# Attention's output projection with fp32 operands instead of split fp16 halves, and the value bias added where the values are spread

## The chip, the cores and the metric

The kernel runs on one core of one Trainium2 chip. The metric is the device time of one launch in microseconds (us), the median of several runs. The engines are named as in the profile: PE (TensorE, its weight loads apart as PEld), DVE (VectorE), ACT (ScalarE), POOL (GpSimd) and SP (SyncE, which here issues all DMAs).

## The reference, cut to what matters

One transformer layer for 32 batch entries of 512 tokens and 256 channels: adaptive layer norm, causal attention with 16 heads of 16 channels and a linear position bias, a gated residual, a second adaptive layer norm, and a gated feed-forward part. The change touches these lines only:

```python
qkv = x @ w_qkv.T + b_qkv
q, k, v = jnp.split(qkv, 3, axis=-1)
...
probs = jax.nn.softmax(scores, axis=-1)
out = jnp.einsum('bhqk,bhkd->bhqd', probs, v)
out = out.transpose(0, 2, 1, 3).reshape(B, S, D)
return out @ w_out.T + b_out
```

The rows of `probs` sum to one, so the value part of `b_qkv` may be added to `v`, or after the division by the softmax sum to the attention's output. The bias is not zero here.

## The kernel before, in words

All 32 batch entries go through one software pipeline written by hand. A batch is called b. One iteration i has 16 slots, one for each head h of batch i, and every engine walks through the same slots in its own instruction stream; semaphores tie the streams together. In iteration i the scores and the exponentials of batch i are made, the row maxima of batch i (heads 8 to 15, slots 0 to 7) and of batch i+1 (heads 0 to 7, slots 8 to 15), the layer norm and QKV product of batch i+1, the output projection of batch i-1 and the feed-forward part of batch i-2. The tables SIDE, SP_AT, DVE_AT, POOL_AT and ACT_AT (L29 to L87) say in which slot each of these side steps stands.

A slot looks like this on the three busiest engines:

- PE (order "01asub2wc", L25): scores in three chunks 0, 1 and 2 (L575, a head's transposed scores for the exponential), row scores in three parts a, b, c (L589, 512, 384+128 and 256 columns, for the row maxima), the side steps s and u, and w, the product of exponentials and values for one key tile of the group of four heads before (L603, L609, fp32).
- DVE (order "SUaboc", L27): the side steps S and U of the slot before, the maxima a and b (L853), the steps o of DVE_AT, then the maxima c.
- ACT: the exponentials (L647) and the evictions of the side products.

The row scores alternate between two PSUM banks (L585), so PE's row scores b of slot t+1 wait until DVE has read the maxima c of slot t (L584), and the row scores c of a slot wait for its maxima a. The side products alternate between two other banks; each waits until the product before it in its bank has been read (L505).

The output projection of batch i-1 is made so. The unnormalised attention output goes through DRAM and comes back as `oc`, the reciprocal sums as `rz`. POOL multiplies them to `om` in slot 9 (`normalise`, L986). In slot 11 ACT writes `oh`, the fp16 rounding of om plus the value bias `bv` (`o_hi`, L714), and DVE writes `ol`, the rest in fp16 (`o_lo`, L868), in its place o, between the maxima b and c. PE makes the product "out" in slots 14 (n = 0) and 15 (n = 1), each with two times six matmuls of 128x128 weights by 256 columns: oh by wo_hi, oh by wo_lo, ol by wo_hi, for two channel halves (L497, called from L548). DVE multiplies it with the gate to `ot` (L799), POOL adds the residual (L1000).

The values: ACT evicts them to `vst` (L684) and POOL spreads them to `va` (`spread`, L976), four heads at a time, into groups of 32 columns of which 16 hold the values and the others the ones for the softmax sum. POOL's order in the slots is: mask of head t (L1018, which zeroes the exponentials above the diagonal), then the steps of POOL_AT: spread of group 2 in slot 1, of group 0 in slot 2, of groups 1 and 3 in slot 3. Ahead of the mask of slot 0 stands norm_c of slot 15 (L965, L969). The step w of slot 4 is the first on head group 0 and waits for the masks of heads 0 to 3 and for a spread (L597 to L599).

Of the kernel before, what the change touches and what calls it, by code (L numbers as in the profile page):

```python
# [7 lines left out]
F32 = mybir.dt.float32  # L8
F16 = mybir.dt.float16
# [5 lines left out]
P = 128  # L15
WS = 16.0
# [48 lines left out]
    11: [("o_lo", None, -1)],  # L65
# [19 lines left out]
    11: [("o_hi", None, -1)],  # L85
# [4 lines left out]
SILU, SILU_T, MOD, ROWS, OW_T, WEIGHTS, MOE = 3, 5, 9, 17, 18, 28, 32  # L90
# [8 lines left out]
def build(nc, x, w_qkv, b_qkv, w_out, b_out, gate_w, expert_w, out_w, cond, wmod,  # L99
# [10 lines left out]
    with ctx:  # L110
# [19 lines left out]
        wo_hi = sb("wo_hi", [P, DC, D], F16)  # L130
        wo_lo = sb("wo_lo", [P, DC, D], F16)
# [5 lines left out]
        bv = sb("bv", [P, DC], F32)  # L137
# [29 lines left out]
        oh = sb("oh", [P, DC, S], F16)  # L167
        ol = sb("ol", [P, DC, S], F16)
# [68 lines left out]
        for name in ("ld_c", "ld_m", "ld_w", "set_dve", "set_pe", "set_act", "set_ready", "rows_stored", "kaug_loaded",  # L237
                     "xa_loaded", "moda_loaded", "lna_stats", "lna_aggr", "lna_ready", "rsa_ready", "xna_ready",
                     "ta_ready", "hfa_ready", "hha_ready", "hla_ready", "qk_ready", "qk_hi", "qk_lo",
                     "qk_stored0", "qk_stored1", "qk_stored2", "qk_stored3", "stack_loaded0", "stack_loaded1",  # L240
                     "stack_loaded2", "stack_loaded3", "masked",
                     "v_ready", "v_evicted", "va_ready", "mx_ready", "mx_read", "mt_ready", "nm_ready",
                     "aug_loaded", "st_ready", "exp_done", "pv_done", "ou_ready", "ou_stored",
                     "zc_loaded", "oc_loaded", "zr_ready", "rz_stored", "rz_loaded", "om_ready", "oh_ready",
                     "ol_ready", "out_ready", "ot_ready", "x1_ready", "xc_loaded", "ga_loaded", "xg_ready",
                     "lnc_stats", "lnc_aggr", "lnc_ready", "rsc_ready", "xnc_ready", "modc_loaded", "gb_loaded",
                     "t2_ready", "hfc_ready", "hhc_ready", "hlc_ready", "gate_ready", "gate_step", "gate_exp",
                     "scl_ready", "moe_ready", "z0_ready", "zs_ready", "zg_ready", "res_ready", "res_stored",
                     "passed_sp", "passed_dve", "passed_pool"):
            sm(name)  # L250
# [63 lines left out]
        def _(sp):  # L314
# [16 lines left out]
            ld("ld_w", bv[:], b_qkv[2 * D:3 * D].rearrange("(c p) -> p c", p=P), allow_slow_non_contiguous=True)  # L331
# [111 lines left out]
        def _(pe):  # L443
# [56 lines left out]
            def side_step(name, n, b, bank, prev):  # L500
# [39 lines left out]
                elif name == "out":  # L540
                    wait(pe, "ol_ready", (b + 1) * 2)
                    for u in range(2):
                        t = slice((2 * n + u) * P, (2 * n + u + 1) * P)
                        pairs = []
                        for c in range(DC):
                            pairs += [(oh[:, c, t], wo_hi[:, c, :]), (oh[:, c, t], wo_lo[:, c, :]),
                                      (ol[:, c, t], wo_hi[:, c, :])]
                        x_ = products(dst[:, u * D:(u + 1) * D], pairs)  # L548
# [88 lines left out]
        def _(act):  # L637
# [71 lines left out]
            def o_hi(b):  # L709
                wait(act, "om_ready", b + 1)  # L710
                wait(act, "out_ready", b * 2)
                wait(act, "ol_ready", b * 2)
                for c in range(DC):
                    nc.scalar.activation(oh[:, c, :], om[:, c, :], ACT.Identity,  # L714
                                         bias=bv[:, c:c + 1]).then_inc(s["oh_ready"], 1)

# [21 lines left out]
            steps = dict(sums_out=sums_out, gate_exp=gate_exp, o_hi=o_hi)  # L738
# [4 lines left out]
        def _(dve):  # L743
# [119 lines left out]
            def o_lo(b):  # L863
                wait(dve, "om_ready", b + 1)
                wait(dve, "oh_ready", b * 2 + 2)
                wait(dve, "out_ready", b * 2)
                for c in range(DC):
                    v.scalar_tensor_tensor(ol[:, c, :], om[:, c, :], bv[:, c:c + 1], oh[:, c, :], ALU.add,  # L868
                                           ALU.subtract).then_inc(s["ol_ready"], 1)

# [5 lines left out]
                invert=invert, o_lo=o_lo)  # L876
# [32 lines left out]
            step(v.tensor_scalar(mrow[:, 0:D], g_abs[:, 0:D], 1.0 / WS, None, ALU.mult))  # L909
# [4 lines left out]
            def split(hi, lo, src):  # L914
# [9 lines left out]
            split(wo_hi[:].rearrange("p c n -> p (c n)"), wo_lo[:].rearrange("p c n -> p (c n)"),  # L924
                  flat[:, 12 * P:16 * P])
# [34 lines left out]
        def _(pool):  # L960
# [11 lines left out]
            def spread(b, g):  # L972

                wait(pool, "v_evicted", (b + 1) * 2, "passed_pool")
                wait(pool, "pv_done", b * 16 - 4 * (3 - g), "passed_pool")
                q.tensor_scalar(va[:, :, 4 * g:4 * g + 4, 0:HD],  # L976
                                vst[:, :, 64 * g:64 * g + 64].rearrange("p t (h d) -> p t h d", h=4),
                                1.0, 0.0, ALU.mult, ALU.add).then_inc(s["va_ready"], 1)

            def normalise(b):  # L980
# [3 lines left out]
                wait(pool, "oh_ready", b * 2, "passed_pool")  # L984
                wait(pool, "ol_ready", b * 2, "passed_pool")
# [90 lines left out]
```

## Time and profile before

| | us |
|---|---|
| median of 3 runs | 1957.38 |
| runs | 1954.21, 1957.84, 1957.38 |
| span of the profiled execution, first to last instruction | 1953.2 |
| granted TensorE clock, mean of the span | 0.977 |
| busy PE / PEld | 1724.6 / 995.6 |
| busy DVE | 1552.6 |
| busy ACT | 1214.8 |
| busy POOL | 998.9 |

The profile shows one execution. Its time with what lies around the span is not listed by itself; the three timed runs lie 1.0 to 4.6 us above its span. A busy PE is not PE at its peak, since a matmul's shown duration contains its way through the array; the distance from one start to the next is what a matmul costs in a dense row. "Idle before" is the time in which an engine did nothing ahead of an instruction, with the instruction that released it.

### The profile page before, as it was taken

The numbers are of one execution on the slowest core, as the hardware profiler recorded it, in microseconds if no ns is written. First come the engines' busy times: TensorE is split into PE (matmuls) and PEld (weight loads), VectorE is DVE, ScalarE is ACT, GpSimd is POOL, SyncE is SP. The second block draws the span as 40 slices with busy tenths as digits, with TensorE's granted clock in tenths as the row PEclk, the third lists the DMA queues.
The fourth block names the chain that finished last, engine by engine and source line by source line (L and its number), as shares of the span: only waits on it lengthen the run. The fifth ranks groups of instructions, "written<-read, shape, count | busy, mean of one in ns | idle before, by whom it ended". The sixth has DMA issues, their size and how long they took to land.

```text
span 1953.2 us, 62334 instructions
## 1 busy us (share of the span) xinstructions
PE 1724.6 (88%) x17744; PEld 995.6 (51%) x17744; DVE 1552.6 (79%) x5632; ACT 1214.8 (62%) x2466; POOL 998.9 (51%) x1225
## 2 busy tenths in 40 slices
PE   5799999998989998999999898999899999999974
PEld 3455555555555455555555555545555555555542
DVE  5778888888888878888888888887888888888843
ACT  1366666666666666666666666666666666666651
POOL 3234555545545455555554554545555545455454
PEclk8799999999999999999999999999999999999986
DMA  4243333433333443333344333344333334433321
GB/s 131 77 133 116 125 119 128 141 128 124 125 104 125 140 136 126 120 125 120 128 141 128 123 125 104 126 141 136 125 120 125 121 129 139 131 123 115 120 88 45
DMA packets 206753, 238.21 MB, mean 122 GB/s; under 512 B 27626, under 2 KB 153138, under 8 KB 206674
## 3 DMA queue, kind: packets, MB, share of 16 engines
q1 hardware_dynamic: 206710, 237.67, 37.3%
q8 instruction: 23, 0.38, 0.1%
q14 instruction: 20, 0.16, 0.0%
HBM read 135.13 MB, written 101.81 MB: 121 GB/s over the span
## 4 chain that ended last, share of the span: by engine, by line
PE 49%; DVE 24%; issue 18%; ACT 4%; DMA 2%; DVEq 2%; POOL 1%; SPq 1%; ACTq 0%; POOLq 0%
PE ps L497 18%; PE ps L589 12%; DVE ps L853 9%; PE ps L575 8%; PE ps L609 4%; PE ps L603 4%; DVE mxt L853 4%; DVE ol L868 2%; DVEq L257 1%; ACT hf_a L658 1%; ACT hh_a L660 1%; DVE qk_st L793 1%; DVE st_c L759 1%; ACT prob L647 1%; PE ps L515 1%
## 5 line engine op out<-in xcount | busy, mean ns | idle before, releaser
L853 DVE CUSTOM_DVE_ANT_0 ps<-ps,mask_qk 128x512 f32<-128x512 f32 (+3 forms) x2048 | 971.1, 510 | 296.3 <-PE ps L589 285.3
L647 ACT ACTIVATE prob<-ps 128x512 f32<-128x512 f32 (+1 forms) x1536 | 743.5, 530 | 363.2 <-PE ps L575 362.3
L589 PE MATMUL ps<-kz,qs 112*128 112x512 f16 (+3 forms) x2048 | 542.4, 307 | 138.2 <-DVE mxt L853 129.5
L1018 POOL TENSOR_SCALAR_AFFINE_SELECT prob<-prob 128x512 f32<-128x512 f32 x512 | 353.4, 696 | 364.2 <-ACT prob L647 364.2
L575 PE MATMUL ps<-qs,kz 114*128 114x128 f16 (+2 forms) x3584 | 453.3, 243 | 3.7 <-DMA qs<-negm 3.1
L589 PEld LDWEIGHTS ps<-kz,qs 112*128 112x128 f16 x2048 | 187.1, 97 | 492.8 <-DVE mxt L853 308.6
L853 DVE DVE_READ_ACCUMULATOR2_ANT mxt<- 128x1 f32 x2048 | 288.6, 141 | 0.0
L575 PEld LDWEIGHTS ps<-qs,kz 114*128 114x128 f16 x3584 | 259.7, 98 | 50.5 <-ACT prob L647 3.8
L609 PE MATMUL ps<-prob,va 128*32 128x384 f32 (+2 forms) x3072 | 237.0, 380 | 0.0
L603 PE MATMUL ps<-prob,va 128*32 128x128 f32 x4096 | 218.3, 285 | 2.0 <-issue 0.9
L679 ACT ACTIVATE qk_st<-ps,bqk 128x512 f16<-128x512 f32 x128 | 88.0, 688 | 97.7 <-PE ps L497 95.7
L992 POOL TENSOR_TENSOR xg<-xc,ga_bc 128x1024 f32<-128x1024 f32 x32 | 75.6, 2361 | 101.6 <-DMA ga_bc<-rows_d 90.5
L986 POOL TENSOR_TENSOR om<-oc,rz 128x1024 f32<-128x1024 f32 x32 | 75.5, 2359 | 95.3 <-DMA rz<-rz_d 95.3
L603 PEld LDWEIGHTS ps<-prob,va 128*32 128x32 f32 x4096 | 81.1, 108 | 84.6 <-issue 81.7
L965 POOL TENSOR_TENSOR rs_c<-ve_c,neg_half 128x4 f32<-128x4 f32 x32 | 32.7, 1022 | 166.4 <-DVE nm_c L774 166.4
L793 DVE SCALAR_TENSOR_TENSOR qk_st<-ps,bqk,qk_st 128x512 f16<-128x512 f32 x128 | 95.6, 747 | 7.1 <-ACT qk_st L679 7.1
L497 PE MATMUL ps<-moe_hi,hh_c 128*128 128x512 f16 x256 | 99.5, 389 | 1.0 <-DVE gsub L826 1.0
L1008 POOL TENSOR_TENSOR zg<-zs,gb_bc 128x512 f32<-128x512 f32 x64 | 81.4, 1271 | 36.1 <-DVE zs L806 35.1
L695 ACT ACTIVATE z<-ps,scl 128x256 f32<-128x256 f32 x128 | 60.5, 473 | 62.9 <-PE ps L497 58.8
L497 PE MATMUL ps<-moe_lo,hh_c 128*128 128x512 f16 x256 | 99.2, 387 | 0.0
L497 PE MATMUL ps<-moe_hi,hl_c 128*128 128x512 f16 x256 | 99.1, 387 | 0.0
L497 PE MATMUL ps<-hh_a,wqkv_hi 128*128 128x512 f16 x256 | 97.9, 382 | 0.4 <-DVE qk_st L793 0.4
(115 smaller groups left out, 2818.7 us busy)
## 6 DMA issues: line engine op xcount, KB each, us to landing
qk_d<-qk_st SPq DMA_DIRECT2D x128, 256.0 KB, 2.0
ou_d<-ou SPq DMA_DIRECT2D x128, 256.0 KB, 2.0
qs<-qk_d SPq DMA_DIRECT2D x128, 192.0 KB, 2.6
kz<-qk_d SPq DMA_DIRECT2D x256, 96.0 KB, 2.6
xa<-in_L_attn_x SPq DMA_DIRECT2D x32, 512.0 KB, 4.3
qk_d<-qk_st SPq DMA_DIRECT2D x128, 128.0 KB, 1.9
xc<-in_L_attn_x SPq DMA_DIRECT2D x32, 512.0 KB, 3.5
oc<-ou_d SPq DMA_DIRECT2D x64, 256.0 KB
```

What stands on the lines that cost most here:

```text
L497: x_ = mm(dst, a, b, start=(n == 0), stop=(n == len(pairs) - 1))
L575: x_ = mm(ps[:, ST + n, col:col + w * P], kz[0:STACK, h, kt * P:(kt + 1) * P], qs[0:STACK, h // 2, qt * P:(qt + w) * P], start=True, stop= ...
L589: x_ = mm(ps[:, bank, col:col + w], qs[0:CONST, h // 2, qt * P:(qt + 1) * P], kz[0:CONST, h, 0:w], start=True, stop=True)
L603: x_ = mm(ps[32 * j:32 * j + 32, PVB, kt * P:(kt + 1) * P], va[:, kt, h, :], prob[:, h % 8, kt * P:(kt + 1) * P], start=(kt == 0), stop=(k ...
L609: x_ = mm(ps[32 * j:32 * j + 32, PVB, (kt + 1) * P:S], va[:, kt, h, :], prob[:, h % 8, PCOL[kt]:PCOL[kt] + w], start=False, stop=False)
L647: nc.scalar.activation(prob[:, h % 8, at:at + w], ps[:, ST + n, 0:w], ACT.Exp, scale=1.0 / FS).then_inc(s["exp_done"], 1)
L679: nc.scalar.activation(qk_st[:, k, 0, :], src, ACT.Identity, bias=bqk[:, 2 * k + n // 2:2 * k + n // 2 + 1]).then_inc(s["qk_hi"], 1)
L793: v.scalar_tensor_tensor(qk_st[:, kk, 1, :], src, bqk[:, 2 * kk + n // 2:2 * kk + n // 2 + 1], qk_st[:, kk, 0, :], ALU.add, ALU.subtract). ...
L853: x_ = v.tensor_tensor_reduce(ps[:, bank, col:col + w], ps[:, bank, col:col + w], mask_qk[:, S - w:S], 1.0, -3e38, ALU.add, ALU.max, mxt[: ...
L992: q.tensor_tensor(xg[:], xc[:], ga_bc[:, 1:2, :].broadcast_to([P, QT, D]), ALU.add).then_inc(s["xg_ready"], 1)
L1008: q.tensor_tensor(zg[:, t, :], zs[:, t, :], gb_bc[:].rearrange("p (o d) -> p o d", o=1).broadcast_to([P, 2, D]), ALU.mult).then_inc(s["zg_ ...
L1018: q.affine_select(out=d, in_=d, compare_op=ALU.is_ge, fill=0.0, base=0, pattern=[[0, 4], [1, P]], channel_multiplier=-1).then_inc(s["maske ...
```

## The change

The output projection takes `om` and a fp32 copy of the weights `wo_f` directly; a product then has two matmuls of fp32 operands in place of six of fp16. The steps o_hi on ACT and o_lo on DVE go, with their tiles and semaphores. PE waits for `om_ready` instead of `ol_ready`; POOL's normalise waits for the product of the batch before (`out_ready`) instead of oh and ol. The value bias is loaded as a row broadcast to all partitions, and spread, a tensor_scalar with one tensor input before, becomes a tensor_tensor that adds this row. At the start, one copy stands for the two steps that split the output weights, and the first gate row is no longer divided by the weight scale.

```diff
-    11: [("o_lo", None, -1)],
...
-    11: [("o_hi", None, -1)],
...
-            ld("ld_w", bv[:], b_qkv[2 * D:3 * D].rearrange("(c p) -> p c", p=P), allow_slow_non_contiguous=True)
+            ld("ld_w", bv_bc[:], b_qkv[2 * D:3 * D].rearrange("(o d) -> o d", o=1).broadcast_to([P, D]))
...
-                    wait(pe, "ol_ready", (b + 1) * 2)
+                    wait(pe, "om_ready", b + 1)
                     for u in range(2):
                         t = slice((2 * n + u) * P, (2 * n + u + 1) * P)
-                        pairs = []
-                        for c in range(DC):
-                            pairs += [(oh[:, c, t], wo_hi[:, c, :]), (oh[:, c, t], wo_lo[:, c, :]),
-                                      (ol[:, c, t], wo_hi[:, c, :])]
+                        pairs = [(om[:, c, t], wo_f[:, c, :]) for c in range(DC)]
                         x_ = products(dst[:, u * D:(u + 1) * D], pairs)
...
-            def o_hi(b):
-                wait(act, "om_ready", b + 1)
-                wait(act, "out_ready", b * 2)
-                wait(act, "ol_ready", b * 2)
-                for c in range(DC):
-                    nc.scalar.activation(oh[:, c, :], om[:, c, :], ACT.Identity,
-                                         bias=bv[:, c:c + 1]).then_inc(s["oh_ready"], 1)
...
-            def o_lo(b):
-                wait(dve, "om_ready", b + 1)
-                wait(dve, "oh_ready", b * 2 + 2)
-                wait(dve, "out_ready", b * 2)
-                for c in range(DC):
-                    v.scalar_tensor_tensor(ol[:, c, :], om[:, c, :], bv[:, c:c + 1], oh[:, c, :], ALU.add,
-                                           ALU.subtract).then_inc(s["ol_ready"], 1)
...
-            step(v.tensor_scalar(mrow[:, 0:D], g_abs[:, 0:D], 1.0 / WS, None, ALU.mult))
+            step(v.tensor_copy(mrow[:, 0:D], g_abs[:, 0:D]))
...
-            split(wo_hi[:].rearrange("p c n -> p (c n)"), wo_lo[:].rearrange("p c n -> p (c n)"),
-                  flat[:, 12 * P:16 * P])
+            step(v.tensor_copy(wo_f[:].rearrange("p c n -> p (c n)"), flat[:, 12 * P:16 * P]))
...
-                q.tensor_scalar(va[:, :, 4 * g:4 * g + 4, 0:HD],
+                bias = bv_bc[:, 64 * g:64 * g + 64].rearrange("p (o h d) -> p o h d", o=1, h=4)
+                q.tensor_tensor(va[:, :, 4 * g:4 * g + 4, 0:HD],
                                 vst[:, :, 64 * g:64 * g + 64].rearrange("p t (h d) -> p t h d", h=4),
-                                1.0, 0.0, ALU.mult, ALU.add).then_inc(s["va_ready"], 1)
+                                bias.broadcast_to([P, QT, 4, HD]), ALU.add).then_inc(s["va_ready"], 1)
...
-                wait(pool, "oh_ready", b * 2, "passed_pool")
-                wait(pool, "ol_ready", b * 2, "passed_pool")
+                wait(pool, "out_ready", b * 2, "passed_pool")
```

## Rows read from the trace of the kernel before

**Rows 1.** The page, part 1: busy time, share of the span, instructions.

```profile
PE 1724.6 (88%) x17744; PEld 995.6 (51%) x17744; DVE 1552.6 (79%) x5632; ACT 1214.8 (62%) x2466; POOL 998.9 (51%) x1225
```

**Rows 2.** The waits: engine, line, awaited; us in total, times, longest.

```profile
PE ps L589 <- DVE mxt L853: 129.5, 200, 4.1
```

**Rows 3.** Groups by form: shapes, count | busy us, mean ns | idle before, releaser.

```profile
L868 DVE SCALAR_TENSOR_TENSOR ol<-om,bv,oh 128x512 f16<-128x512 f32 x64 | 89.7, 1440 | 5.0 <-ACT oh L714 5.0
...
L1008 POOL TENSOR_TENSOR zg<-zs,gb_bc 128x512 f32<-128x512 f32 x64 | 81.4, 1271 | 36.1 <-DVE zs L806 35.1 <-issue 1.0
...
L992 POOL TENSOR_TENSOR xg<-xc,ga_bc 128x1024 f32<-128x1024 f32 x32 | 75.6, 2361 | 101.6 <-DMA ga_bc<-rows_d 90.5 <-issue 11.1
...
L976 POOL TENSOR_SCALAR va<-vst 128x256 f32<-128x256 f32 x128 | 50.7, 405 | 0.9 <-PE ps L603 0.9
...
L714 ACT ACTIVATE oh<-om,bv 128x512 f16<-128x512 f32 x64 | 42.7, 714 | 23.1 <-POOL om L986 23.0
...
L916 DVE SCALAR_TENSOR_TENSOR wo_lo<-ps,wo_hi 128x512 f16<-128x512 f32 x1 | 0.7, 691 | 0.0
```

**Rows 4.** DVE in time, slots 11 to 13, o_lo an iteration later: start, us.

```profile
1021.76 2.89 DVE L868 SCALAR_TENSOR_TENSOR ol<-om,bv,oh 128x512 f16<-128x512 f32 x2
1024.57 0.42 DVE L853 CUSTOM_DVE_ANT_0 ps<-ps,mask_qk 128x256 f32<-128x256 f32 x1
...
1025.92 0.59 DVE L853 CUSTOM_DVE_ANT_0 ps<-ps,mask_qk 128x384 f32<-128x384 f32 x1
...
1026.68 1.39 DVE L759 BATCH_NORM_STATS2 st_a<-xa 128x6 f32<-128x256 f32 x4
1028.00 0.41 DVE L853 CUSTOM_DVE_ANT_0 ps<-ps,mask_qk 128x256 f32<-128x256 f32 x1
...
1079.49 1.85 DVE L868 SCALAR_TENSOR_TENSOR ol<-om,bv,oh 128x512 f16<-128x512 f32 x1
```

**Rows 5.** PE in time, slots 12 and 13.

```profile
1023.26 0.38 PE L497 MATMUL ps<-moe_hi,hl_c 128*128 128x512 f16 x1
1025.11 0.39 PE L589 MATMUL ps<-kz,qs 112*128 112x384 f16 x2 [1.47 <-DVE mxt L853]
...
1028.53 0.39 PE L589 MATMUL ps<-kz,qs 112*128 112x384 f16 x2 [0.60 <-DVE mxt L853]
```

**Rows 6.** POOL in time, the masks of heads 11 and 12.

```profile
1023.02 2.12 POOL L1018 TENSOR_SCALAR_AFFINE_SELECT prob<-prob 128x512 f32<-128x512 f32 x2
```

**Rows 7.** PE in time: product "out" of slot 14, first and last of 12.

```profile
1030.53 0.27 PE L497 MATMUL ps<-wo_hi,oh 128*128 128x256 f16 x1
...
1031.73 0.27 PE L497 MATMUL ps<-wo_hi,ol 128*128 128x256 f16 x1
```

**Rows 8.** PE in time: fp32 matmuls of the start, short windows, three pending each.

```profile
38.42 0.81 PE L490 MATMUL ps<-vst,prob 128*128 128x256 f32 x3
...
38.64 0.81 PE L490 MATMUL ps<-vst,prob 128*128 128x256 f32 x3
```

**Rows 9.** One iteration by window: stretch, busy of five engines, granted clock, DMA.

```profile
980.20:1037.90 57.70, 52.52 (x553) 30.35 (x552) 47.74 (x176) 37.82 (x78) 30.84 (x39) 1.00 0.37 126
```

**Rows 10.** POOL in time, slots 1 to 3 (spread, mask).

```profile
993.87 0.41 POOL L976 TENSOR_SCALAR va<-vst 128x256 f32<-128x256 f32 x1
...
995.20 0.64 POOL L1018 TENSOR_SCALAR_AFFINE_SELECT prob<-prob 128x512 f32<-128x512 f32 x1
```

**Rows 11.** PE in time, slot 4: the step w.

```profile
996.12 0.42 PE L603 MATMUL ps<-prob,va 128*32 128x128 f32 x8
```

**Rows 12.** In time near the end: PE released by POOL.

```profile
1897.87 2.16 POOL L969 TENSOR_SCALAR xn_c<-x,nm_c,rs_c 128x256 f32<-128x256 f32 x4
...
1900.17 0.66 PE L515 MATMUL ps<-ident,xn_c 128*128 128x128 f32 x2 [4.97 <-POOL xn_c L969]
```

**Rows 13.** In time: the last batch's output projection.

```profile
1912.74 2.35 POOL L986 TENSOR_TENSOR om<-oc,rz 128x1024 f32<-128x1024 f32 x1 [2.90 <-DMA rz<-rz_d]
...
1919.71 0.40 PE L497 MATMUL ps<-wo_hi,oh 128*128 128x256 f16 x1 [5.30 <-DVE zs L806]
```

More of the change, by code:

```diff
@@ L88 @@
 C_LOADS, M_LOADS, W_LOADS = 2, 2, 9
-SILU, SILU_T, MOD, ROWS, OW_T, WEIGHTS, MOE = 3, 5, 9, 17, 18, 28, 32
+SILU, SILU_T, MOD, ROWS, OW_T, WEIGHTS, MOE = 3, 5, 9, 17, 18, 27, 31
 PE_SILU_T, PE_MOD, PE_TURNED, PE_MOE = 1, 2, 3, 4
@@ L129, in build @@
         wqkv_lo = sb("wqkv_lo", [P, DC, 3 * D], F16)
-        wo_hi = sb("wo_hi", [P, DC, D], F16)
-        wo_lo = sb("wo_lo", [P, DC, D], F16)
+        wo_f = sb("wo_f", [P, DC, D], F32)
         moe_hi = sb("moe_hi", [P, DC, 2 * D], F16)
@@ L136, in build @@
         bqk = sb("bqk", [P, 4], F32)
-        bv = sb("bv", [P, DC], F32)
+        bv_bc = sb("bv_bc", [P, D], F32)
         modT = sb("modT", [P, NB, 8], F32)
@@ L166, in build @@
         om = sb("om", [P, DC, S], F32)
-        oh = sb("oh", [P, DC, S], F16)
-        ol = sb("ol", [P, DC, S], F16)
         xc = sb("xc", [P, QT, D], F32)
@@ L243, in build @@
                      "aug_loaded", "st_ready", "exp_done", "pv_done", "ou_ready", "ou_stored",
-                     "zc_loaded", "oc_loaded", "zr_ready", "rz_stored", "rz_loaded", "om_ready", "oh_ready",
-                     "ol_ready", "out_ready", "ot_ready", "x1_ready", "xc_loaded", "ga_loaded", "xg_ready",
+                     "zc_loaded", "oc_loaded", "zr_ready", "rz_stored", "rz_loaded", "om_ready", "out_ready", "ot_ready", "x1_ready", "xc_loaded", "ga_loaded", "xg_ready",
                      "lnc_stats", "lnc_aggr", "lnc_ready", "rsc_ready", "xnc_ready", "modc_loaded", "gb_loaded",
@@ L736, in one @@
                                 side_step(name, n, b, bank)
-            steps = dict(sums_out=sums_out, gate_exp=gate_exp, o_hi=o_hi)
+            steps = dict(sums_out=sums_out, gate_exp=gate_exp)
             iterations(act, one)
@@ L875, in _ @@
                 aggregate_c=aggregate(st_c, mv_c, ve_c, nm_c, ("lnc_stats", "lnc_aggr", "lnc_ready"), "xnc_ready", "rsc_ready"),
-                invert=invert, o_lo=o_lo)
+                invert=invert)
             dve.wait_ge(s["ld_c"], C_LOADS * 16)
```

## The prediction

> **What bounds the kernel now.** I read the page first, then the waits, then one iteration in order of time. On the page PE is busy for 88% of the span and DVE for 79% [rows 1], which names no single bound; the order of work inside a slot decides. The waits show where the two meet: PE's row scores wait for DVE's maxima 200 times, 129.5 us in all [rows 2]. In order of time the middle of the run repeats exactly: o_lo starts at 1021.76 and again at 1079.49, a period of 57.73 us [rows 4], at full granted clock [rows 9]. So the change can be costed for one period and multiplied by the number of iterations in which it applies. About 30 of them are full (the product "out" of batches 0 to 29 stands beside row maxima of a next batch), one more is the last with scores, and one is the tail.
>
> The largest wait of PE within a period is in slot 12, and o_lo makes it. DVE starts o_lo at 1021.76 and needs 2.89 us for its two halves; only then, at 1024.57, come the maxima c of slot 11 [rows 4]. PE has issued its last feed-forward matmul at 1023.26 and could issue the row scores b at about 1023.26 + 0.22 = 1023.48 (0.22 is the distance of two such matmuls, see the fp32 rows below for the same distance); it does so at 1025.11, released by DVE [rows 5]. The 2.89 us are more than the work: a half of o_lo has a mean of 1440 ns [rows 3], and the masks that POOL makes at that time take 2.12 us for two [rows 6] where one takes 0.64 elsewhere [rows 10]. The two engines hold each other up there.
>
> **What goes.**
>
> *o_lo on DVE.* Without it the maxima c of slot 11 start at 1021.76 and are read before 1022.3, so the row scores b of slot 12 go at 1023.48, 1.63 us earlier. What is late next on DVE is the maxima b of slot 12. Today they start at 1025.92 [rows 4], held by DVE's own backlog. They would start when their scores arrive: 1023.48, plus 0.39 for the matmuls [rows 5], plus some 0.2 us until DVE sees them, 1024.05, which is 1.87 us earlier. Behind them stand the four statistics of the next layer norm, 1.39 us, and the maxima c, at 1028.00 today [rows 4], and these release PE's row scores b of slot 13 at 1028.53 [rows 5]. That chain is DVE's own work from end to end and moves as a whole: minus 1.87 us per period. From slot 13 on, PE's own row is the limit (product "out", values, product "out"), and it moves with it. Could POOL take over as the bound in slot 12? The step w there needs the mask of head 11. That mask starts at 1023.02 [rows 6]; without a rival on DVE it lasts 0.64, to 1023.66, and w would be issued at about 1023.9. It fits by a tenth. If it did not, PE would wait a little in w and less before the row scores b of slot 13, for which the DVE chain is later anyway. So I take 1.87. Its bounds: 1.63, if nothing beyond the first wait is won, and 2.2, the 1.47 + 0.60 us of the two waits [rows 5] and what lies in between.
>
> *o_hi on ACT.* 2 x 714 ns per batch [rows 3]. Nobody waits for ACT in slots 11 and 12 in the rows of PE or DVE; the exponentials behind it come earlier and are not awaited. Zero in the period. If that cover were gone the most it could give is its 1.33 us.
>
> **What comes on PE.** Twelve matmuls of a product stand at 1030.53 to 1031.73, 0.109 us apart, so 1.31 us [rows 7]. The nearest rows for the new form are exact in shape: the fp32 matmuls of the start, 128x128 weights by 256 columns. There each matmul of the program is two instructions, and they start 0.22 us apart, at 38.42 and 38.64, with three pending [rows 8] (0.215 from four such steps). Four matmuls of a product are eight instructions, 1.72 us: plus 0.41 for each of the two products. PE has no idle time around either, so it all counts: plus 0.82. In slot 15 the product follows matmuls 0.109 apart, which may not hide the first longer fp32 weight load: plus 0.08. Together plus 0.90, between 0.82 and, if the clock were at its lower level of 1.2 GHz there, 0.90 + 3.4; the clock reads 1.00, its level of 2.4 GHz, throughout the period [rows 9], and less waiting of PE gives no reason for it to fall. I take 0.90.
>
> The new wait of PE, `om_ready`, is met: om is finished at 1019.1 and the product stands at 1030.53 [rows 7], over 9 us later even when 1.87 us come off. Behind this wait are all row scores of slots 14 and 15, so it would be dear if it were not met. POOL's new wait in normalise asks for the product of the batch before, 37 us old by then; om is overwritten only 37 us after its last reader. Both cost nothing. SP's queue is moved past nothing; its steps wait for the same events as before.
>
> **What comes on POOL.** The spread gets a second tensor input. It takes 405 ns now [rows 3]. The trace has no such add over 256 elements. Its nearest rows are two-input operations of POOL on 512 and 1024 elements, 1271 and 2361 ns [rows 3]: a line through them has 2.13 ns per element and 181 ns at zero, so 726 ns for 256. The lower bound is no change, 405 ns; the upper is the whole 1271 ns of the 512 form, if runs of 16 elements with a broadcast operand cost the double. I take 0.73, nearest to the line: plus 0.32 for each spread.
>
> Whether that counts depends on what follows. From 993.87 on POOL runs without a pause through spread 2, mask 2, spread 0 and mask 3, which ends at 995.84 [rows 10]; PE's w of slot 4, which needs mask 3, is issued at 996.12 [rows 11]. From POOL's end to PE's start it takes 0.14 us (1897.87 + 2.16 = 1900.03, then 1900.17 [rows 12]), so the slack is only 0.14. Two spreads stand ahead of that mask: 2 x 0.32 - 0.14 = plus 0.50 per period, as a new wait of PE in front of w. Nothing later absorbs it: behind w are the row scores c, DVE waits for them, and DVE's maxima a of slot 5 hold the row scores c in turn. The other two spreads stand behind mask 3 and delay only the mask of head 4, needed in slot 8: zero. It applies in the 31 iterations from the second on, in which norm_c stands ahead of the masks.
>
> On this the Trainium skill speaks against the change: "GPSIMD Engine Reference", section on elementwise cycle accounting, gives a two-input tensor_tensor about 2.6 cycles per element at 1.2 GHz and a one-input operation as little as 1.0 to 1.8. By its 4497 ns for 2048 elements a spread would be an estimated 562 ns, and the total gain about 10 us larger; its slope, 2.17 ns, agrees with the 2.13 of the trace.
>
> **Start and end.** At the start one DVE step of 0.69 us [rows 3] drops out of the chain that PE waits for: minus 0.7. In the tail, where nothing else runs, om ends at 1915.1 and the product starts at 1919.71 [rows 13]; o_hi, o_lo and what queued behind them lie in between. The product would start some 4.5 us earlier and, with 16 instructions by 0.215 to 0.43 for 24 by 0.213, last 1.7 us less to 1.8 longer: minus 4. In the last iteration with scores DVE has no row maxima and ACT is the limit, o_hi's 1.33 us against PE's 0.90: minus 0.4.
>
> **The sum.** 30 x (-1.87 + 0.90) = -29.1; 31 x 0.50 = +15.5; start, end and last iteration -5.1. Together -18.7 us: the span goes from 1953.2 to 1934.5. The timed runs lie 1.0 to 4.6 above the span before, the median 4.2. Against the median, 1957.4 - 18.7 = 1938.7; I say 1938.
>
> **The rivals.**
>
> *A, the longer spread is hidden.* If the add costs about as little as the multiply now, or POOL reaches slot 1 earlier than in this trace, the 15.5 us do not come: 1957.4 - 34.2 = 1923. For it: at 0.47 us per spread the slack would cover both. Against it: no two-input row of POOL is near that. The middle ground, some 0.56 us per spread, gives 1928.
>
> *B, the spread becomes the bound (slower).* The add writes runs of 16 elements and reads a broadcast row; if POOL needs 1.27 us for it, w of slot 4 waits 2 x 0.87 - 0.14 = 1.6 us in each of 31 periods, 49.6 us, against a gain of 34.2: +15, 1973. It decides from the point where 31 x (2x - 0.14) = 34.2, x = 0.62 us more per spread, so a spread of 1.03 us. For it: POOL has no slack at all between norm_c and mask 3. Against it: today's spread has the same runs and is no slower per element than the plain forms.
>
> *C, fp32 weight loads aren't hidden (slower).* 16 loads with 0.09 us more each that count, 1.4 us per period, 45 us: 1983. Against it: the loads of the start were of this kind and the matmuls still stood 0.22 apart [rows 8].
>
> *D, the wait moves.* PE's waits in slots 12 and 13 give only the first 1.63, or POOL's mask of head 11 holds w: 7 to 12 us less gain, 1946 to 1950.
>
> **How the numbers follow.** Forecast 0.48, A and its middle ground 0.20, D 0.11, B 0.14 (half of it around the break-even), C and others 0.07. The range reaches from A, with 2 us for the spread of runs, over D to the break-even of B: 1921 to 1958; some 0.15 are left out above and 0.05 below. A measurement of this kernel tells about 0.2%, 4 us, from no change: faster by more 0.75, within 0.11, slower by more 0.14.
>
> **What would show it.** In the changed profile: the wait of row scores b in slot 12 gone and that in slot 13 still there with about 0.5 us; fp32 instructions of the product 0.215 us apart, 1.72 us per product; a spread of 0.73 us; a new wait in front of w of slot 4 of about half a microsecond, released by POOL's mask; masks of head 11 back at 0.64; a period of 57.73 - 1.87 + 0.90 + 0.50 = 57.26. A spread above 1.03 us, or a period above 57.7, makes the prediction wrong.

## The result, and the profile after

The changed kernel takes 2142.78 us (median of 4 runs, 2137.66 to 2147.13) against 1957.61 us for the kernel before on the same chip (4 runs, 1954.21 to 1958.01): ratio 1.0948, 95% interval 1.0929 to 1.0967. It is 9.5% slower where 1% faster was forecast, and far outside the range. The span goes from 1953.2 to 2140.2 us.

The page of the changed kernel, parts 1 to 3 (busy time by engine, granted TensorE clock in tenths over 40 slices, instruction queue), part 4 (shares of the chain that ended last) and one group of part 5 (busy us, mean ns | idle before, releaser):

```profile
PE 1802.7 (84%) x17488; PEld 1047.1 (49%) x17488; DVE 1471.0 (69%) x5567; ACT 1189.3 (56%) x2402; POOL 1020.2 (48%) x1225
...
PEclk8899999999999999999999999999999999999996
...
q14 instruction: 155, 1.27, 0.2%
...
PE 52%; issue 21%; DVE 17%; POOL 4%; DMA 2%; ACT 2%; DVEq 1%; SPq 1%; POOLq 0%; ACTq 0%
...
L782 DVE TENSOR_TENSOR ot<-ps,ga_bc 128x512 f32<-128x512 f32 x64 | 44.1, 688 | 178.4 <-issue 163.4
```

DVE did what the change says: 82 us less busy time than in [rows 1]. Yet no engine is nearer to its bound; all are less busy as a share. The time is idle time, and one row holds most of it: in front of `ot` DVE stood still for 163.4 us, and what ended that is "issue", that is, nothing the profile shows. The waits of DVE in the changed kernel count 28 pauses (us in total, times, longest), and those of PE show whom they hit:

```profile
DVE ot L782 <- issue: 163.4, 28, 6.6
```

```profile
PE ps L504 <- DVE ot L782: 169.9, 28, 6.8
PE ps L580 <- DVE mxt L836: 68.7, 142, 4.1
...
PE ps L594 <- POOL prob L992: 10.2, 28, 1.1
```

The second and third of these lines are the ones the prediction spoke of: PE's wait for the maxima fell from 129.5 us in 200 waits [rows 2] to 68.7 in 142, and the new wait in front of w is there, 28 times. The first line is new and larger than all of them.

One of the 28 pauses is short, 0.17 us at 174.0, ahead of the counted loop. The other 27 last 5.5 to 6.6 us. The loop makes 28 passes, so it jumps back 27 times, and all 27 long pauses have the same place: right behind the jump back. DVE in order of time in the changed kernel (start, us, ..., [idle before <-releaser]):

```profile
1136.99 0.47 DVE L836 CUSTOM_DVE_ANT_0 ps<-ps,mask_qk 128x256 f32<-128x256 f32 x1
1137.37 0.14 DVE L836 DVE_READ_ACCUMULATOR2_ANT mxt<- 128x1 f32 x1
1143.37 0.69 DVE L782 TENSOR_TENSOR ot<-ps,ga_bc 128x512 f32<-128x512 f32 x1 [5.85 <-issue]
```

The same place in the kernel before:

```profile
1038.35 0.47 DVE L853 CUSTOM_DVE_ANT_0 ps<-ps,mask_qk 128x256 f32<-128x256 f32 x1
1038.73 0.14 DVE L853 DVE_READ_ACCUMULATOR2_ANT mxt<- 128x1 f32 x1
1039.00 0.69 DVE L799 TENSOR_TENSOR ot<-ps,ga_bc 128x512 f32<-128x512 f32 x1
```

Between these rows lie only control instructions, which no view prints but whose records the trace has. In the kernel before, DVE's jump is at 1038.44 and its next instruction 0.27 us later. In the changed one the jump is at 1137.07, the next instruction at 1140.56, 3.5 us later, and behind three instructions there is a second hole, until 1143.37. In each of the two holes lies one packet of the queue "instruction" (the DMA view of the changed kernel, first for 1137.1 to 1140.6, then for 1140.6 to 1143.4: packets, MB, share; the third is one whole period, 1078.0 to 1142.5):

```profile
q14 instruction: 1, 0.01, 1.1%
...
q14 instruction: 1, 0.01, 1.3%
...
q14 instruction: 5, 0.04, 0.2%
```

Five packets of 8192 bytes in every period; in the kernel before there is none between 226.0 and 1803.4 us, and 20 in all. DVE fetches its loop anew in every pass, and twice it has to stand and wait for the fetch.

PE feels it with a delay: it needs `ot` read out of its bank before the transposes of the next layer norm go on. PE in order of time in the changed kernel, then the windows ahead of, around and behind the hole (stretch; busy of five engines; granted clock; DMA):

```profile
1137.42 0.60 PE L504 MATMUL ps<-ident,xn_a 128*128 128x128 f32 x4
1144.11 1.12 PE L504 MATMUL ps<-ident,xn_a 128*128 128x128 f32 x4 [6.09 <-DVE ot L782]
```

```profile
1101.50:1136.50 35.00, 32.92 (x320) 19.37 (x319) 25.68 (x101) 19.11 (x41) 18.64 (x21) 1.00 0.38 109
1136.50:1148.00 11.50, 5.40 (x44) 2.99 (x41) 3.85 (x15) 4.83 (x9) 2.21 (x2) 0.70 0.31 93
1148.00:1166.00 18.00, 16.52 (x193) 9.35 (x192) 15.63 (x58) 13.09 (x26) 10.74 (x16) 1.00 0.42 137
```

While PE stands, the clock falls from its level of 2.4 GHz to that of 1.2: it reads 0.50 in every stretch from 1141 to 1147 us, 0.70 as a mean of the 11.5 us. The four transposes behind the wait take 1.12 us; the same four take 0.66 in the kernel before. So slot 0 lasts 11.6 us (3.85 before), nearly 7.8 more: some 5.8 by the idle row, the rest on the way out at the lower clock. (Slots are measured in the trace from the start of a head's scores on PE to that of the next head's; all slot times here are medians over the batches.) The period is 64.6 us for 57.73.

The other fifteen slots are 0.9 us shorter in sum, so what the prediction had costed did happen; it is read below in a kernel without the holes.

### The profile page after: what moved, and what is told of

It is laid out like the page before. It is cut to its first block, busy times and chain, and to the rows that moved or that the text cites. A ratio compares the mean times of both kernels' runs of the same rounds, so it can differ in the third digit from the quotient of the medians.

```text
span 2140.2 us, 61543 instructions
## 1 busy us (share of the span) xinstructions
PE 1802.7 (84%) x17488; PEld 1047.1 (49%) x17488; DVE 1471.0 (69%) x5567; ACT 1189.3 (56%) x2402; POOL 1020.2 (48%) x1225
## 3 DMA queue, kind: packets, MB, share of 16 engines
q14 instruction: 155, 1.27, 0.2%
## 4 chain that ended last, share of the span: by engine, by line
PE 52%; issue 21%; DVE 17%; POOL 4%; DMA 2%; ACT 2%; DVEq 1%; SPq 1%; POOLq 0%; ACTq 0%
PE ps L491 18%; PE ps L580 12%; PE ps L566 8%; DVE ps L836 6%; PE ps L600 6%; PE ps L594 5%; DVE mxt L836 3%; POOL va L951 2%; DVE ot L782 2%; POOL prob L992 2%; PE ps L504 1%; PE ps L532 1%; DVEq L251 1%; DMA kz<-qk_d 1%; DVE st_a L742 1%
## 5 line engine op out<-in xcount | busy, mean ns | idle before, releaser
L580 PE MATMUL ps<-kz,qs 112*128 112x512 f16 (+3 forms) x2048 | 553.8, 313 | 79.4 <-DVE mxt L836 68.7
L992 POOL TENSOR_SCALAR_AFFINE_SELECT prob<-prob 128x512 f32<-128x512 f32 x512 | 335.8, 663 | 300.5 <-ACT prob L638 300.2
L566 PE MATMUL ps<-qs,kz 114*128 114x128 f16 (+2 forms) x3584 | 464.9, 247 | 3.2 <-DMA qs<-negm 2.7
L600 PE MATMUL ps<-prob,va 128*32 128x384 f32 (+2 forms) x3072 | 254.8, 405 | 0.0
L504 PE MATMUL ps<-ident,xn_a 128*128 128x128 f32 x256 | 52.4, 343 | 172.8 <-DVE ot L782 169.9
L974 POOL TENSOR_TENSOR x<-ot,xg 128x512 f32<-128x512 f32 x64 | 81.1, 1268 | 209.0 <-DVE ot L782 208.7
L782 DVE TENSOR_TENSOR ot<-ps,ga_bc 128x512 f32<-128x512 f32 x64 | 44.1, 688 | 178.4 <-issue 163.4
L649 ACT ACTIVATE hf_a<-ps,mod_a 128x512 f32<-128x512 f32 x64 | 49.8, 779 | 181.6 <-PE ps L504 178.9
L491 PE MATMUL ps<-wo_f,om 128*128 128x256 f32 x512 | 124.7, 388 | 3.9 <-POOL om L960 3.9
L504 PEld LDWEIGHTS ps<-ident,xn_a 128*128 128x128 f32 x256 | 35.0, 173 | 182.4 <-DVE ot L782 176.8
```

What stands on the lines that cost most here:

```text
L491: x_ = mm(dst, a, b, start=(n == 0), stop=(n == len(pairs) - 1))
L504: x_ = nc.tensor.transpose(dst[:, t * P:(t + 1) * P], xn_a[:, t, n * P:(n + 1) * P], ident[:])
L566: x_ = mm(ps[:, ST + n, col:col + w * P], kz[0:STACK, h, kt * P:(kt + 1) * P], qs[0:STACK, h // 2, qt * P:(qt + w) * P], start=True, stop= ...
L580: x_ = mm(ps[:, bank, col:col + w], qs[0:CONST, h // 2, qt * P:(qt + 1) * P], kz[0:CONST, h, 0:w], start=True, stop=True)
L600: x_ = mm(ps[32 * j:32 * j + 32, PVB, (kt + 1) * P:S], va[:, kt, h, :], prob[:, h % 8, PCOL[kt]:PCOL[kt] + w], start=False, stop=False)
L782: v.tensor_tensor(ot[:, 2 * n:2 * n + 2, :], src.rearrange("p (u d) -> p u d", u=2), ga_bc[:, 0:1, :].broadcast_to([P, 2, D]), ALU.mult).t ...
```

## The experiments

**Is it the place of the loop in DVE's program?** Theory: instructions are fetched in blocks, and whether DVE's loop stays loaded from pass to pass depends on how many blocks it touches. Counted in the traces' records, DVE has 447 instructions ahead of its loop and 325 in it before, 443 and 321 after. Of the four that are gone ahead of the loop, three are o_lo of the one iteration there that has it, one is the start's split step. The packets are 8192 bytes. How many instructions that is can be estimated from a second queue "instruction", q8: it moved 23 packets of 16384 bytes in either kernel, and PE's program, with its loop counted once, has 5932 instructions before; if that queue is PE's, which no view says, an instruction has some 64 bytes, and a packet of 8192 bytes holds 128. Before, the loop lay in three blocks; after, four instructions fewer ahead of it move its start over a block's edge, so that it lies in four. Rival: what the loop contains (fp32 product, new waits) makes the holes. The edit leaves the loop as it is and puts N tiny instructions at the very start of DVE's program:

```
+        pad = sb("pad", [P, N], F32)
...
+            for n in range(N):
+                v.memset(pad[:, n:n + 1], 0.0)
```

N = 8, after_pad8:

> The changed kernel with 8 tiny memsets more at the very start of DVE's stream; nothing else differs. Theory F (instruction fetch): in the changed trace DVE's loop starts 3 instructions ahead of the end of an 8 KB block of instructions, so that its 321 instructions touch four blocks, and after each branch back the blocks have to be fetched again; 8 instructions more move the start behind the boundary, the loop touches three, no fetch is left inside the loop, and the time falls to 1925 to 1940 us, period about 57.0. Rival W (a data wait: ot behind ga, x1 or the product): the eight memsets change nothing, 2140 us. Rival S (the longer spread and the fp32 products are what costs): 2140 us too.

1946.05 us (5 runs, 1942.98 to 1948.07), ratio 0.9936 [0.9921, 0.9951]. Eight instructions of no use took 196.7 us away: 7.3 us for each of the 27 jumps back. The queue on the page of this kernel, and its group of `ot` (busy, mean ns | idle before, releasers):

```profile
q14 instruction: 21, 0.16, 0.0%
```

```profile
L783 DVE TENSOR_TENSOR ot<-ps,ga_bc 128x512 f32<-128x512 f32 x64 | 44.1, 689 | 18.5 <-PE ps L492 15.0 <-POOL x L977 0.2
```

The row of "issue" is gone, and the 155 packets are 21. Slot 0 is back at 3.85 us. The rival is out, as the loop is the same. The measured time lies a little above the expected one; where that comes from is read below.

N = 1, after_pad1, to see that it is not the padding as such:

> The same with 1 memset. F: the loop still starts ahead of the boundary (2 instructions in place of 3), still four blocks, 2135 to 2150 us. If any change of the layout of the start heals it, by chance and not by the boundary, it would be near 1935 like the one with 8.

2142.75 us, ratio 1.0942 [1.0919, 1.0966], 155 packets: nothing changed in the time, as expected. But one thing moved, and it shows where the edge is: in the changed kernel the second hole stands behind three instructions after the jump (443 and three), in after_pad1 behind two (444 and two). So the edge lies behind the 446th recorded instruction of DVE's program, and with blocks of 128 the next ones lie behind the 574th, 702nd and 830th. Before, the loop goes from 447 to 772 and touches three blocks; after, from 443 to 764, four; in after_pad8, from 451 to 772, three.

N = 80, after_pad80, and the kernel before with N = 90, before_pad90, to put the end of the loop over an edge instead of its start (523 to 844, and 537 to 862):

> The same with 80 memsets. F: the loop starts 77 instructions into a block and needs 77 + 321 = 398 > 384, four blocks again, so it stalls again; but 51 instructions lie ahead of the next boundary, enough to hide the second fetch, so only the first stall of some 3.3 us stays: about 2030 to 2060 us. If what counts is only that the start is not close to a boundary: about 1940.

> The kernel before with 90 memsets at the start of DVE's stream. F: its loop starts about one instruction behind a boundary, 91 with the memsets, and 91 + 325 = 416 > 384: four blocks, one stall of some 3.3 us in each of 28 passes, 2045 to 2075 us, with instruction fetches inside the loop that it has not now. Rivals W and S, which sit in the change: 1957 to 1965 us.

2052.52 us, ratio 1.0482 [1.0459, 1.0505], and 2066.21 us, ratio 1.0552 [1.0531, 1.0573]. The page of after_pad80, queue and group of `ot`:

```profile
q14 instruction: 157, 1.28, 0.2%
...
L783 DVE TENSOR_TENSOR ot<-ps,ga_bc 128x512 f32<-128x512 f32 x64 | 44.1, 689 | 101.4 <-issue 88.9
```

And the waits of DVE in before_pad90 (its queue has 156 packets):

```profile
DVE ot L800 <- issue: 87.0, 27, 3.9
```

The kernel before, untouched but for ninety small instructions ahead of everything, loses 5.5%. That is the plainest proof that no part of the change's own work is needed for the loss. Five packets a pass here too, but only one hole of 3.2 to 3.3 us (87.0 / 27, 88.9 / 27): the second block is loaded in time. The whole cost is some 4 us per jump back (106.5 us against after_pad8, over 27), a little over half of the changed kernel's. The clock falls here too: 0.949 as a mean of the span of after_pad80, 0.932 in the changed kernel, 0.978 in after_pad8. The second hole comes where only the last two or three instructions of a block belong to the loop, so that the next block is needed at once (the changed kernel and after_pad1), and is missing where 51 (after_pad80) or 37 (before_pad90) stand ahead of the edge. How many it takes between 3 and 37 was not measured.

**What does the longer spread cost?** after_pad8 has a period of 57.47 us; the forecast was 57.26. Two slots grew: slot 4 from 3.63 to 4.05, slot 5 from 2.84 to 3.30. In order of time in after_pad8, PE, POOL and DVE:

```profile
993.24 0.42 PE L595 MATMUL ps<-prob,va 128*32 128x128 f32 x8 [0.35 <-POOL prob L995]
...
997.54 0.28 PE L581 MATMUL ps<-kz,qs 112*128 112x256 f16 x1 [0.80 <-DVE mxt L837]
```

```profile
990.58 0.73 POOL L954 TENSOR_TENSOR va<-vst,bv_bc 128x256 f32<-128x256 f32 x1
991.25 0.64 POOL L995 TENSOR_SCALAR_AFFINE_SELECT prob<-prob 128x512 f32<-128x512 f32 x1
991.86 0.73 POOL L954 TENSOR_TENSOR va<-vst,bv_bc 128x256 f32<-128x256 f32 x1
992.54 0.64 POOL L995 TENSOR_SCALAR_AFFINE_SELECT prob<-prob 128x512 f32<-128x512 f32 x1
993.15 1.43 POOL L954 TENSOR_TENSOR va<-vst,bv_bc 128x256 f32<-128x256 f32 x2
...
995.63 0.64 POOL L995 TENSOR_SCALAR_AFFINE_SELECT prob<-prob 128x512 f32<-128x512 f32 x1 [0.47 <-ACT prob L639]
```

```profile
995.06 1.75 DVE L765 TENSOR_TENSOR hl_c<-hf_c,hh_c 128x512 f16<-128x512 f32 x2
```

The first wait is the forecast one: the mask ends at 993.18, w goes at 993.24. The second was not forecast. A mask of POOL starts at 995.63, the second half of DVE's `hl_c` at 995.66, and the pair of `hl_c` takes 1.75 us where 1.29 is usual: that half is held for the mask's 0.64 us, and PE's row scores c wait for the maxima behind it. Theory P: both slots, 0.88 us per period, are the spreads' work. Three kernels take it away in three ways. pad8_spread1 leaves the value bias out and has the old one-input spread:

```
-                q.tensor_tensor(va[:, :, 4 * g:4 * g + 4, 0:HD],
...
+                q.tensor_scalar(va[:, :, 4 * g:4 * g + 4, 0:HD],
...
+                                1.0, 0.0, ALU.mult, ALU.add).then_inc(s["va_ready"], 1)
```

> The changed kernel with 8 memsets, but spread is again the one-input multiply, so the value bias is left out. Theory P (the longer spread costs 0.88 us per period: 0.42 as PE's new wait for mask 3 in slot 4, 0.46 as DVE's hl_c held up by mask 4 in slot 5, both read from the run with 8 memsets): 1946 - 31 x 0.88 = 1919 us, slot 4 back at 3.63, slot 5 at 2.84. The record's term of 0.50 alone: 1946 - 15.5 = 1930 us. Rival (the longer spread is hidden, the loss against the forecast lies elsewhere): 1946 us.

1924.59 us (1920.04 to 1931.16), ratio 0.9837 [0.9812, 0.9862], period 56.59, slots 4 and 5 at 3.63 and 2.84. pad8_moved keeps the add and moves three of the four spreads behind the masks that PE waits for:

```
-    1: [("spread", 2, 0)],
...
-    3: [("spread", 1, 0), ("spread", 3, 0)],
+    5: [("spread", 1, 0), ("spread", 2, 0)],
+    6: [("spread", 3, 0)],
```

> The changed kernel with 8 memsets and the two-input spread, but only the spread of group 0 ahead of mask 3 (slot 2), those of groups 1 and 2 in slot 5, group 3 in slot 6. P: PE's wait in slot 4 and DVE's hold-up in slot 5 both go although the spread is as long as before: 1946 - 27 = 1919 us. If the length of POOL's work as such were the cost: 1946.

1924.24 us (1922.02 to 1924.68), ratio 0.9823 [0.9807, 0.9838], period 56.60, the same slots as pad8_spread1. So the add is free where nobody waits behind it; its place alone makes it dear. fold_bias takes the bias out of the loop altogether: since each head's probabilities sum to one, b_v reaches the output as b_v W_o, which it multiplies out once at the start with the fp32 weights and adds to the constant row of the output projection. Five memsets and its own steps put DVE's loop behind 452 instructions, in three blocks.

```
+                for c in range(DC):
+                    x_ = mm(ps[0:NB, PVB, 0:D], bv_nb[:, c, :], wo_f[:, c, :], start=(c == 0), stop=(c == DC - 1))
...
+                step(v.tensor_tensor(bo_bc, ps[0:NB, PVB, 0:D], bo_bc, ALU.add))
+                step(v.tensor_tensor(mrow[:, D:2 * D], g_abs[:, 0:D], bo_bc, ALU.mult))
```

> A version that should beat both: no bias in spread (one input); the value bias goes through the output weights once at the start (two matmuls on PE, two DVE steps) into the bias row of the gated residual, since the rows of probs sum to one; 5 memsets and 3 steps place DVE's loop behind the block boundary. P: as without the bias, 1919 us, plus 1 to 3 us for the start: 1919 to 1924. If the place of the loop is missed: over 2040.

1917.5 us (5 runs, 1915.75 to 1921.73), ratio 0.9802 [0.9787, 0.9816]: 2% faster than the kernel before with all of the computation in it, period 56.59. This is the best version found.

**Is that cost the spread's own?** before_spread2 puts the adding spread into the kernel before, without the fp32 product; o_hi and o_lo no longer add the bias:

```
-                    v.scalar_tensor_tensor(ol[:, c, :], om[:, c, :], bv[:, c:c + 1], oh[:, c, :], ALU.add,
+                    v.scalar_tensor_tensor(ol[:, c, :], om[:, c, :], 1.0, oh[:, c, :], ALU.mult,
...
-                q.tensor_scalar(va[:, :, 4 * g:4 * g + 4, 0:HD],
...
+                q.tensor_tensor(va[:, :, 4 * g:4 * g + 4, 0:HD],
```

> One part of the change alone: the kernel before with the two-input spread that adds the bias; o_hi and o_lo stay, without the bias. DVE's stream keeps its length. P: plus 31 x (0.42 to 0.88) = 1970 to 1984 us against 1957. Rival (what makes the spread cost is that other work moved earlier): 1957.

1957.39 us, ratio 0.9998 [0.9988, 1.0007]. Theory P missed, and its rival had the right time. But the slots say something else than "hidden": slot 4 did grow, 3.63 to 4.03, and slot 12 shrank, 5.32 to 4.79. The edit had changed a second thing, the form of o_lo. POOL in order of time in the kernel before, beside o_lo at 1021.76 [rows 4]:

```profile
1021.80 1.27 POOL L1012 TENSOR_TENSOR res<-zg,x 128x512 f32<-128x512 f32 x1 [0.34 <-POOL zg L1008]
```

The same place in before_spread2, DVE and then POOL:

```profile
1021.50 2.37 DVE L867 SCALAR_TENSOR_TENSOR ol<-om,oh 128x512 f16<-128x512 f32 x2
```

```profile
1021.53 1.79 POOL L1012 TENSOR_TENSOR res<-zg,x 128x512 f32<-128x512 f32 x1 [0.34 <-POOL zg L1008]
```

In the kernel before, POOL's `res` keeps its 1.27 us and the first half of o_lo is held for it (1.86 us, the second half 1.11). In before_spread2 it is the other way: the first half takes 0.69, `res` is held to 1.79, and only the second half waits (1.76). The pair is 0.52 us shorter.

And slot 5 kept its 2.84, since there mask and `hl_c` met with the other outcome, the mask held to 1.19 us and the pair of `hl_c` at its usual 1.29 (POOL, then DVE):

```profile
998.28 1.19 POOL L1018 TENSOR_SCALAR_AFFINE_SELECT prob<-prob 128x512 f32<-128x512 f32 x1 [0.51 <-ACT prob L647]
```

```profile
997.69 1.29 DVE L780 TENSOR_TENSOR hl_c<-hf_c,hh_c 128x512 f16<-128x512 f32 x2
```

Two kernels take the two edits apart. before_spread3 has the adding spread and the old form of o_lo, with a column of zeros for `bv`; before_ol1 has only the new form of o_lo (it leaves the bias out of the low half).

> The kernel before with the value bias added where the values are spread, as in the kernel called before_spread2, but with o_lo on VectorE kept in its old form (a column operand, here all zeros, instead of the constant 1.0). In before_spread2 the spread cost 0.40 us in slot 4, and slot 12 was 0.53 us shorter since the pair of o_lo instructions took 2.37 us instead of 2.89. Theory Q (the spread costs 0.40 us per period whatever else is there, and the change of form of o_lo hid it): period 57.73 + 0.40 = 58.13, 1957.4 + 31 x 0.40 = about 1970 us, 1966 to 1973, with slot 12 back at 5.3 us. Rival (the later GpSimd work, not the form of o_lo, shortens slot 12): slot 12 stays at 4.8 us and the time at 1957.

1969.01 us (6 runs, 1967.37 to 1983.07), ratio 1.0046 [1.0030, 1.0063]: as theory Q says. The runs fall into two groups, four at 1967.4 to 1969.1 and two at 1981.9 and 1983.1; the profiled one is of the second, with slot 4 at 4.05, slot 12 at 5.31 and also slot 5 at 3.30, since in it the race is lost again:

```profile
1013.24 1.75 DVE L781 TENSOR_TENSOR hl_c<-hf_c,hh_c 128x512 f16<-128x512 f32 x2
```

The two groups are 14 us apart, and 31 x 0.46 = 14.3. So it looks as if `hl_c` was not held in the four short runs; only one run of this kernel has a trace, so this is inferred from their times. What decides the race can be read from six traces that hold it (after, after_pad1, after_pad8, after_pad80, before_spread2, before_spread3). The mask starts first in nearly all of them, by the recorded starts. Where it is ahead by 20 ns or more (20 to 41, and once 19), `hl_c` is held; where it is ahead by 2 to 19 ns, or starts 41 to 55 ns behind, the mask is. In the changed kernel both happen within one execution: leads of 4 to 15 ns 22 times, of 20 to 27 ns five times. So it is not chance that decides, but some 0.02 us of start.

> The kernel before with one edit: o_lo on VectorE is (o times the constant 1.0) minus o_hi instead of (o plus the bias column) minus o_hi. It leaves out the value bias in the low half alone. Theory Q (the form of the instruction is what shortened slot 12 in before_spread2): slot 12 about 4.8 us instead of 5.32, period 57.2, 1957.4 - 31 x 0.53 = about 1941 us, 1938 to 1945. Rival (timing against GpSimd's masks and residual shortened it): 1955 to 1959, slot 12 at 5.3 us.

1941.56 us (1940.05 to 1945.70), ratio 0.9917 [0.9900, 0.9934], slot 12 at 4.79, all others as before: the form of o_lo alone is worth 0.8%. Theory Q holds for the time; of its rival the mechanism is right, since what the form changes is who is held. Unhindered, the new form is only 0.06 us shorter (0.69 for 0.75). `res` starts some 0.03 us behind the first half of o_lo in both kernels (medians 32 and 34 ns); with the new form that half keeps its 0.69 us in 29 of 32 iterations, with the old one it takes some 1.8 us or more in 28. Together the two edits of before_spread2 come to a period of 57.60, 0.13 shorter than before, so some 1953; the profiled run took 1953.9, the median of the ten 1957.4, and where the others lose the difference stays open.

**Is the hidden spread fully hidden?** fold_moved is fold_bias with the spreads also moved as in pad8_moved.

> The changed kernel with the bias folded into the output projection's constant row at the start (the spreads go back to their one-input form, 0.405 us) and the spreads at other slots: group 0 in slot 1, groups 1 and 2 in slot 5, group 3 in slot 6. The kernels fold_bias, pad8_moved and pad8_spread1 all ended at a period of 56.59 us with slots 4 and 5 at 3.63 and 2.84 us. If the spreads are fully hidden in all three (theory), moving them once more gives nothing: period 56.6 us, 1915 to 1925 us, the same as fold_bias within 0.3%. If the spread of 0.405 us still cost something in slots 4 and 5 (rival: the 3.63 us of slot 4 is set by it), slot 4 falls below 3.6 us and the time below 1912 us.

1919.56 us (1915.91 to 1920.63), ratio 0.9800 [0.9783, 0.9816], period 56.60, slot 4 at 3.63: the same as fold_bias. The one-input spread costs nothing where it stands.

## Why the prediction was wrong

Its sum had no term for the place of the program in memory. The step that failed is the first: "what goes" was read as work only, and an instruction that goes from ahead of an engine's loop also moves that loop. Four instructions of DVE went there. Three are o_lo of an iteration that is written out ahead of the loop, and by the edge found above (447 less three is 444, short of 446) they alone suffice; the start's step, costed at minus 0.7 us, would not have by itself (446). They cost 196.7 us, 27 jumps back by 7.3 us, against all costed terms together of 19. Nothing in the rows of before warned of it as such; what could have been read is that the loop's fetch is free there (20 packets, none in the loop) and that this is a condition that an edit can break.

With the holes taken away (after_pad8), term by term:

- *o_lo off DVE*, -1.87 us forecast. Slots 12 and 13 went from 5.32 and 3.20 to 3.68 and 2.96: -1.88. The row scores b of slot 12 wait no more; those of slot 13 wait 0.35 us, where about 0.5 was said and [rows 5] have 0.60. Right, and rival D is out. In addition slot 7 became 0.12 shorter (5.21 to 5.09), which was not forecast. It is not the work of the change: the slot has 5.09 in before_pad90 too, whose loop is that of the kernel before. Its cause stays open.
- *Masks back at 0.64*: POOL's masks fell from a mean of 696 to 639 ns, so the two engines no longer hold each other there. Right.
- *fp32 product*, +0.90. Product "out" is now one row of eight instructions from 1031.75 on, in after_pad8:

```profile
1031.75 1.89 PE L492 MATMUL ps<-wo_f,om 128*128 128x256 f32 x8
1033.48 0.38 PE L581 MATMUL ps<-kz,qs 112*128 112x384 f16 x2
```

  1.73 us from start to start, 1.72 forecast; slots 14 and 15 grew by 0.45 and 0.42, +0.87. Right, and rival C is out.
- *The spread*: 736 ns in the mean of 128, where the line through two rows of POOL gave 726. Right; the trace's own slope was a better guide than the estimate of 562 ns from the Trainium skill's "GPSIMD Engine Reference", elementwise cycle accounting. Rivals A and B are out by the same number.
- *The new wait in front of w*: +0.50 forecast, +0.42 measured. Right in kind, a bit too large.
- *What was missing in that term*: the two spreads behind mask 3 were called free because they "delay only the mask of head 4, needed in slot 8". The masks behind them came later too, and one now starts together with `hl_c` of DVE. The prediction had named just this sort of mutual hold-up for o_lo (it put it on the masks; the first half is held by `res`, as the rows above show), and looked only for who waits for the mask, not whom it meets on the way: +0.46 per period, +14 us where that race is lost.
- *Start and end*, -5.1 forecast. In the tail of after_pad8 PE's product follows om at once; from om's end to the end of the span it is 35.8 us (1910.4 to 1946.2) for 38.1 (1915.1 to 1953.2): -2.3 where -4 was said. The product starts 4.5 us earlier, as forecast, but lasts 6.53 us for 5.30, at a granted clock of 0.55.

Without the holes the forecast of 1938 would have been 8 us short of the 1946.05 of after_pad8, within its range; without the holes and with the spreads in a better place the change gives 1924. The change is good by its work, and loses by four instructions.

The Trainium skill has a warning that bears on this ("Runtime: NRT & Kernel Launch", instruction fetch mechanics): a taken branch to a target outside the window of pages held forces a fetch before execution can go on. The trace agrees with the mechanism: 3.5 us from the jump to the next instruction, with one packet in between. The section speaks of pages of 16 KiB, two of them. Packets of that size are in the trace, the 23 of q8; those in DVE's holes have 8192 bytes, and for DVE the measurement decides. If four blocks of that size are held and one is always fetched ahead, a loop in three blocks stays and one in four can't, which is what all placements show; the number held was not measured by itself.

## What to carry to other kernels

Any edit that adds or removes instructions ahead of or in a counted loop moves that loop in each engine's program: after every change look at the packets of the instruction queue (20 or 155) and at "issue" idle time of the first instruction behind the jump, before you explain a difference by the work; a few idle instructions ahead of the loop give the time back. Put added work of a helper engine behind, not ahead of, what the bounding engine waits for, and look at what each shifted instruction then runs beside. A change of place can be worth as much as the change itself, and an experiment that changes two things at once can show "no effect" for an effect of 0.6%.

## What the runs showed of the hardware

- Instruction fetch: a loop of 321 or 325 DVE instructions costs nothing in one placement, some 4 us per jump back in another (one hole of 3.3 us), 7.3 us in a third (two holes, 3.5 and 2.5 us), with the clock at its lower level for part of each pass in both. Instructions that do nothing, ahead of the loop, decide: none or one is slow, eight is fast, eighty slow again. The second hole moves with them, instruction by instruction (three behind the jump, then two), so the edge is fixed in the program. PE's loop of 1211 or 1227 instructions fetches nothing in the loop, if q8 is its queue: no packet between 222.7 and 1980.3 us in the changed kernel.
- DVE and POOL hold each other up in whole instructions: of a 128x512 subtraction on DVE (0.69 us alone) and a mask on POOL (0.64 alone) that start within 0.03 us of each other, one takes its usual time and the other most of the sum of 1.33, DVE's `hl_c` 1.15 or POOL's mask 1.19. So with o_lo and `res`: 1.86 and 1.27, or 0.69 and 1.79. Between `hl_c` and the mask a lead of the mask of some 20 ns decides: from there on `hl_c` is held (63 cases in six traces), below it the mask, though it starts first (72 cases).
- Who is held can hang on the form of one instruction: o_lo with a constant operand in place of a column from memory, 0.06 us shorter by itself, has a mean of 1214 ns for 1440 over 64, and the kernel gains 16 us. How much of this is the operand and how much is `mult` for `add` was not set apart.
- In a wait of 6.09 us on PE the granted clock falls to 0.50, its level of 1.2 GHz, and reads so until 3 us behind the wait (1147 us); the mean of the 11.5 us around it is 0.70.
- fp32 matmuls of 128x128 by 256 run as two instructions 0.215 us apart, and their weight loads (194 ns each) stay hidden.
